# Edge-weighted sums of a graph network on one core: GpSimd makes the target one-hots, ScalarE weighs the rows

## The chip, the cores and the metric

One core of a Trainium2 chip runs the whole program. The metric is the device time in microseconds (us). The kernel before was timed in three runs: 6406.73, 6428.13 and 6429.01, median 6428.13.

## The reference, cut to the sums that the change touches

A four-layer graph network over 6250 nodes with 128 features and 106250 directed edges (100000 drawn plus 6250 self-loops), the edges sorted by target node. The change touches the edge sums of the second layer (L1) only. Cut to what matters there:

```python
edge_feat = jnp.concatenate([x[row], x[col]], axis=-1)
h = jax.nn.gelu(edge_feat @ mlp_w1 + mlp_b1, approximate=False)
edge_weight = jax.nn.sigmoid(h @ mlp_w2 + mlp_b2)[:, 0]
...
deg = jax.ops.segment_sum(ew_f, col_f, num_segments=n)
dinv = jnp.where(deg > 0, jax.lax.rsqrt(deg), 0.0)
norm = dinv[row_f] * ew_f * dinv[col_f]
xt = x @ conv_w
msg = xt[row_f] * norm[:, None]
out = jax.ops.segment_sum(msg, col_f, num_segments=n)
```

Here `row_f` and `col_f` are the edges' sources and targets with the self-loops behind, and `ew_f` their weights. The edge pass before it has computed each edge's weight (`score`) and each node's `dinv`, and has written the gathered rows `xt[row_f]` in edge order to DRAM (`spill`). What is left for the edge sums is, for every edge, weight times `dinv` of its source times its row, added up by target node. The factor `dinv` of the target is applied later, in the node phase.

## The kernel before, in words

Phases follow each other with a barrier between: node phase, attention, node phase, edge pass, `weighted_sums("sum1")` (L901 to L1082), node phase, two plain sums (`convolve`), and so on. `weighted_sums` is called once. The edges lie in 832 tiles of 128 edges; TB = 8 tiles make a batch, so there are 104 batches. One partition holds one edge of a tile. Every engine runs its own list of instructions, and only semaphores order them.

For each batch n:

- **SP** loads the batch's rows from `spill` (L949, 512 KB, three buffers, each free again when `s_wrow` says that its rows have been weighed) and a line with the low seven bits of the source indices, broadcast to all partitions (L941, 256 KB, four buffers, freed by `s_lo`).
- **VectorE** makes a one-hot of those low bits (`low_onehot`, L1027, one instruction for the batch). It is done one batch ahead.
- **TensorE** looks up `dinv` of each source (`look_up`, L981): 24 small bf16 matmuls of the low one-hot with a table of `dinv`, split in three bf16 parts, into `pS`. It is done one batch ahead of the sums.
- **VectorE** picks the right column for each edge (`find`, L1037, eight instructions that also write an accumulated value) and multiplies it by the edge's weight (`weigh_edges`, L1049, "the wedge"; eight values per partition).
- **GpSimd** multiplies the rows by the wedge (L962, one product of 128x1024, into `wrow`). In the first seven batches it also scales the nodes' own rows (`keep`, L967).
- **ScalarE** makes the one-hots of the target nodes (`hot`): eight squares of iota minus the edge's local target (L1012) and then relu(1 - square) over the batch (L1016).
- **TensorE** multiplies (`sum_up`, L993): eight fp32 matmuls of `wrow` with `hot` into `pA`, one for each tile; each shows as two instructions in the trace.
- **VectorE** adds the eight results into `acc` at an address that is read from `base` (`add`, L1057). The adds of batch n-2 stand between the finds of batch n, and each add waits for the one before it (`s_add`). The eight addresses are loaded into registers in front (L1073).

`hot`, `wrow`, `pA`, `hot_lo`, `pS`, `found` and `wedge` have two buffers each. So GpSimd and ScalarE may start on batch n only when the sums of n-2 are done (`s_sum`), and TensorE's sums of n only when the adds of n-2 are done. TensorE's order is look_up(n+1), sum_up(n). VectorE's order in step n is low_onehot(n+1), the address load, eight pairs of find(n) and add(n-2), weigh_edges(n). At the start GpSimd clears `acc` (L955), and VectorE splits `dinv` and the source indices in a chain of seven instructions (L1061 to L1067).

## Time and profile before

| | |
|---|---|
| runs, us | 6406.73, 6428.13, 6429.01 |
| the profiled execution, us | 6410.54 |
| its span, us | 6408.8 |
| stage of the edge-weighted sums, us | about 2475 to 2971 |
| TensorE busy in the span | 3755.1 us (59%) |
| VectorE busy in the span | 3524.7 us (55%) |
| ScalarE busy in the span | 2305.3 us (36%) |
| GpSimd busy in the span | 4226.4 us (66%) |
| mean granted TensorE clock | 0.624 |

The span is the time from the first to the last instruction of the profiled execution; its own time is 1.7 us more. In the rows, L962 is a line of the kernel, PE is TensorE's matmuls and PEld its weight loads, DVE is VectorE, ACT ScalarE, POOL GpSimd and SP the engine that issues most DMAs. A tile such as `wrow` shows as `sum_wrow`. In a row of the timeline the square bracket holds how long the engine was idle before it and what ended that time. The granted clock is 1 at 2.4 GHz and 0.5 at 1.2 GHz. Instructions of one engine overlap a little, so durations can add up to more than the busy time.

### The profile page before, as it was taken

The page shows a single profiled execution, that of the slowest core. Times are in us where ns is not written, and L with a number is a line of the kernel's source. Part 1 is how long each engine was busy: PE and PEld are TensorE (multiplying, and loading weights), DVE is VectorE, ACT ScalarE, POOL GpSimd, SP SyncE. Part 2 cuts the span into 40 slices and gives each one's busy share as a digit, 9 for nine tenths or more (in the row PEclk, how much of TensorE's full clock was granted, in tenths as well). Part 3 has the DMA queues.
Part 4 walks back from the last instruction along what each step waited for, and adds up shares of the span by engine and source line. Part 5 has one row for each costly group of instructions (what it writes and reads, how often), then busy time and mean ns, then how long its engine had stood idle before and what let it go on. Part 6 is the DMA issues. An engine that isn't in the chain of part 4 may idle for free. (4 is left out here: it accounts for less than half of the span.)

```text
span 6408.8 us, 85037 instructions
## 1 busy us (share of the span) xinstructions
PE 3755.1 (59%) x21906; PEld 3499.1 (55%) x21906; DVE 3524.7 (55%) x11783; ACT 2305.3 (36%) x5100; POOL 4226.4 (66%) x4385
## 2 busy tenths in 40 slices
PE   4555555457777776666344444544444456888886
PEld 2555555447777776666333333433333346778776
DVE  4777777655555556886333333333333345666665
ACT  3555555344444445786000000100000026666663
POOL 2777777337777775442777777477777737777773
PEclk8777777656666667898555555655555565555556
DMA  5555555125555555552222222122222213333332
GB/s 152 160 159 160 159 159 160 48 68 156 155 153 156 156 155 156 167 181 87 54 53 53 53 53 53 52 53 53 53 53 53 53 43 61 58 59 59 59 59 49
DMA packets 734950, 621.88 MB, mean 97 GB/s; under 512 B 345701, under 2 KB 625721, under 8 KB 734521
## 3 DMA queue, kind: packets, MB, share of 16 engines
q0 software_dynamic: 159744, 356.39, 21.2%
q1 hardware_dynamic: 574776, 260.77, 15.2%
q8 instruction: 148, 2.42, 0.2%
q14 instruction: 282, 2.30, 0.1%
HBM read 532.40 MB, written 84.29 MB: 96 GB/s over the span
## 5 line engine op out<-in xcount | busy, mean ns | idle before, releaser
L1109 POOL DMA_INDIRECT sum_rows<-tab_row,src_idx x1664 | 1570.0, 944 | 656.4 <-issue 506.4
L1121 PE MATMUL sum_pA<-sum_hot,sum_rows 128*128 128x128 f32 x3328 | 851.2, 437 | 1245.5 <-DVE sum_hot L1131 1149.2
L1121 PEld LDWEIGHTS sum_pA<-sum_hot,sum_rows 128*128 128x128 f32 x3328 | 740.9, 328 | 1355.7 <-DVE sum_hot L1131 1269.4
L1153 DVE TENSOR_TENSOR acc<-acc,sum_pA 128x128 f32 x1664 | 480.8, 289 | 1346.1 <-PE sum_pA L1121 1178.5
L618 POOL DMA_INDIRECT l_rows<-tab_qv,src_idx x832 | 791.0, 951 | 368.4 <-issue 247.4
L618 POOL DMA_INDIRECT l_rows<-tab_wh,src_idx x832 | 787.2, 946 | 349.9 <-issue 249.4
L353 POOL DMA_INDIRECT l_rows<-tab_ax,src_idx x832 | 790.6, 950 | 291.6 <-issue 266.1
L668 PE MATMUL l_pA<-l_hotA,l_wrow 128*128 128x128 f32 x3328 | 708.9, 382 | 58.9 <-DVE acc L854 57.8
L640 PE MATMUL l_pK<-l_winr,l_hotT 128*128 128x128 f32 (+1 forms) x3328 | 665.7, 339 | 69.5 <-DVE l_logit L762 49.2
L640 PEld LDWEIGHTS l_pK<-l_winr,l_hotT 128*128 128x128 f32 x3328 | 636.4, 284 | 80.6 <-issue 52.8
L668 PEld LDWEIGHTS l_pA<-l_hotA,l_wrow 128*128 128x128 f32 x3328 | 641.7, 286 | 70.2 <-issue 40.2
L854 DVE TENSOR_TENSOR acc<-acc,l_pA 128x128 f32 x1664 | 474.1, 285 | 234.1 <-PE l_pA L668 177.2
L697 ACT ACTIVATE l_hot<-iota,local 128x128 bf16<-128x128 f32 x1664 | 525.9, 388 | 13.9 <-PEq L75 13.9
L371 PE MATMUL l_pK<-l_winr,l_hotT 128*128 128x64 f32 x1664 | 339.0, 388 | 237.9 <-ACT l_hotT L410 237.9
L715 ACT ACTIVATE l_hotA<-l_hot 128x512 f32<-128x512 bf16 x416 | 259.6, 624 | 584.1 <-PE l_pA L668 579.0
L371 PEld LDWEIGHTS l_pK<-l_winr,l_hotT 128*128 128x128 f32 x1664 | 320.9, 296 | 255.4 <-ACT l_hotT L410 130.0
L1354 ACT ACTIVATE mid_hT<-mid_pH 128x512 f32<-128x512 f32 x7 | 4.2, 597 | 1078.6 <-PE mid_pH L1311 1078.6
L1329 ACT ACTIVATE gat_rss<-gat_rss 128x7 f32<-128x7 f32 x7 | 1.4, 205 | 1069.7 <-DVE gat_rss L1407 1069.7
L962 POOL TENSOR_TENSOR sum_wrow<-sum_rows,sum_wedge 128x1024 f32<-128x1024 f32 x104 | 214.7, 2064 | 257.0 <-DVE sum_wedge L1049 239.4
L993 PE MATMUL sum_pA<-sum_hot,sum_wrow 128*128 128x128 f32 x1664 | 244.5, 308 | 167.1 <-issue 88.2
L451 DVE TENSOR_TENSOR l_pre<-l_rows,l_pK 128x512 f32<-128x512 f32 x104 | 71.5, 688 | 487.3 <-DMA l_rows<-tab_ax,src_idx 481.6
L993 PEld LDWEIGHTS sum_pA<-sum_hot,sum_wrow 128*128 128x128 f32 x1664 | 224.8, 217 | 175.6 <-issue 174.9
(257 smaller groups left out, 7099.9 us busy)
## 6 DMA issues: line engine op xcount, KB each, us to landing
l_winr<-tab_k SPq DMA_DIRECT2D x832, 64.0 KB
spill<-l_rows SPq DMA_DIRECT2D x104, 512.0 KB
sum_rows<-spill SPq DMA_DIRECT2D x104, 512.0 KB
l_winr<-tab_b SPq DMA_DIRECT2D x840, 32.0 KB
sum_line<-src_lo SPq DMA_DIRECT2D x104, 256.0 KB
sum_rows<-tab_row,src_idx POOLq DMA_INDIRECT x1664
l_rows<-tab_qv,src_idx POOLq DMA_INDIRECT x832
l_rows<-tab_ax,src_idx POOLq DMA_INDIRECT x832
```

The lines of the kernel that those rows point to most:

```text
L353: nc.gpsimd.indirect_dma_start(rows[:, b * TB + u, :], None, table, bass.IndirectOffsetOnAxis(src_idx[:, t:t + 1], 0)).then_inc(s_rows[b], 16)
L371: last = nc.tensor.matmul(pK[:, b, u, :], hotT[:, b, u, :], winr[:, b * TB + u, :], start=True, stop=True)
L618: nc.gpsimd.indirect_dma_start(rows[:, g % R, u, :], None, table, bass.IndirectOffsetOnAxis(src_idx[:, t:t + 1], 0)).then_inc(s_rows[g % R ...
L640: last = nc.tensor.matmul(pK[:, g % 2, u, :], hotT[:, g % 2, u, :], winr[:, g % WR, u, :], start=True, stop=True)
L668: last = nc.tensor.matmul(pA[:, g % 2, u, :], wrow[:, g % 2, u, :], hotA[:, g % 2, u, :], start=True, stop=True)
L697: last = nc.scalar.activation(hot[:, g % HR, u, :], iota[:], ACT.Square, scale=-1.0, bias=local[:, t:t + 1])
L715: nc.scalar.activation(hotA[:, g % 2], hot[:, g % HR], ACT.Copy).then_inc(s_hotA, 1)
L854: nc.vector.tensor_tensor(acc[:, bass.ds(at[u], P)], acc[:, bass.ds(at[u], P)], pA[:, g % 2, u, :], ALU.add).then_inc(s_add, 1)
L993: last = nc.tensor.matmul(pA[:, b, u, :], wrow[:, b, u, :], hot[:, b, u, :], start=True, stop=True)
L1109: nc.gpsimd.indirect_dma_start(rows[:, g % R, u, :], None, tab_row, bass.IndirectOffsetOnAxis(src_idx[:, t:t + 1], 0)).then_inc(s_rows[g % ...
L1121: last = nc.tensor.matmul(pA[:, g % HOTS, u, :], rows[:, g % R, u, :], hot[:, g % HOTS, u, :], start=True, stop=True)
L1153: nc.vector.tensor_tensor(acc[:, bass.ds(at, P)], acc[:, bass.ds(at, P)], pA[:, g % HOTS, u, :], ALU.add).then_inc(s_add, 1)
```

## The change

Five things are changed, all in `weighted_sums`. GpSimd makes the target one-hots, with eight compares (iota equal to the local target) per batch, instead of weighing the rows. ScalarE weighs the rows, with eight scaled copies per batch, instead of making the one-hots. `hot`, `wrow` and `pA` have three buffers instead of two. The adds run three batches behind the finds instead of two, in 107 steps instead of 106. The lookups and the low one-hots run two batches ahead instead of one; the low one-hot now follows the wedge in VectorE's step. The seven `keep` products come in batches 3 to 9 instead of 0 to 6.

```diff
@@ -902,10 +902,10 @@
 
             with Phase(nc) as cx:
                 L = name + "_"
-                RB, LB = 3, 4
-                hot = sb(L + "hot", [P, 2, TB, P], fp32, cx)
+                RB, LB, SB = 3, 4, 3
+                hot = sb(L + "hot", [P, SB, TB, P], fp32, cx)
                 rows = sb(L + "rows", [P, RB, TB, F], fp32, cx)
-                wrow = sb(L + "wrow", [P, 2, TB, F], fp32, cx)
+                wrow = sb(L + "wrow", [P, SB, TB, F], fp32, cx)
                 line = sb(L + "line", [P, LB, TB * P], bf16, cx)
                 hot_lo = sb(L + "hot_lo", [P, 2, TB * P], bf16, cx)
                 picked = sb(L + "picked", [P, 2, TB, NB], fp32, cx)
@@ -915,7 +915,7 @@
                 hi_f = sb(L + "hi_f", [P, T], fp32, cx)
                 part = sb(L + "part", [P, 3, NB], bf16, cx)
                 rest = sb(L + "rest", [P, 2, NB], fp32, cx)
-                pA = ps(cx, L + "pA", [P, 2, TB, P])
+                pA = ps(cx, L + "pA", [P, SB, TB, P])
                 pS = ps(cx, L + "pS", [P, 2, TB, F // 2])[:, :, :, 0:NB]
                 s_rows = [sem(cx, L + f"s_rows{b}") for b in range(RB)]
                 s_line = [sem(cx, L + f"s_line{b}") for b in range(LB)]
@@ -925,7 +925,6 @@
                 s_found = sem(cx, L + "s_found")
                 s_wedge = sem(cx, L + "s_wedge")
                 s_wrow = sem(cx, L + "s_wrow")
-                s_square = sem(cx, L + "s_square")
                 s_hot = sem(cx, L + "s_hot")
                 s_sum = sem(cx, L + "s_sum")
                 s_add = sem(cx, L + "s_add")
@@ -954,17 +953,17 @@
                     def _(pool):
                         nc.gpsimd.memset(acc[:], 0.0).then_inc(s_add, 1)
                         for n in range(BATCHES):
-                            b = n % 2
-                            pool.wait_ge(s_wedge, n + 1)
-                            pool.wait_ge(s_rows[n % RB], 16 * (n // RB + 1))
-                            if n >= 2:
-                                pool.wait_ge(s_sum, n - 1)
-                            nc.gpsimd.tensor_tensor(wrow[:, b], rows[:, n % RB],
-                                                    wedge[:, b].unsqueeze(2).to_broadcast([P, TB, F]), ALU.mult
-                                                    ).then_inc(s_wrow, 1)
-                            if n < GROUPS:
-                                own = keep[:, n * GB:(n + 1) * GB, :]
-                                nc.gpsimd.tensor_tensor(own, own, dinv[:, n * GB:(n + 1) * GB].unsqueeze(2)
+                            if n >= SB:
+                                pool.wait_ge(s_sum, n - SB + 1)
+                            for u in range(TB):
+                                t = n * TB + u
+                                last = nc.gpsimd.tensor_scalar(hot[:, n % SB, u, :], iota[:], local[:, t:t + 1], None,
+                                                               ALU.is_equal)
+                            last.then_inc(s_hot, 1)
+                            if SB <= n < SB + GROUPS:
+                                i = n - SB
+                                own = keep[:, i * GB:(i + 1) * GB, :]
+                                nc.gpsimd.tensor_tensor(own, own, dinv[:, i * GB:(i + 1) * GB].unsqueeze(2)
                                                         .to_broadcast([P, GB, F]), ALU.mult).then_inc(s_scaled, 1)
                         pool.wait_ge(s_scaled, GROUPS)
 
@@ -984,11 +983,11 @@
 
                         def sum_up(n):
 
-                            b = n % 2
+                            b = n % SB
                             pe.wait_ge(s_hot, n + 1)
                             pe.wait_ge(s_wrow, n + 1)
-                            if n >= 2:
-                                pe.wait_ge(s_add, 1 + TB * (n - 1))
+                            if n >= SB:
+                                pe.wait_ge(s_add, 1 + TB * (n - SB + 1))
                             for u in range(TB):
                                 last = nc.tensor.matmul(pA[:, b, u, :], wrow[:, b, u, :], hot[:, b, u, :],
                                                         start=True, stop=True)
@@ -996,25 +995,23 @@
 
                         pe.wait_ge(s_split, 7)
                         look_up(0)
+                        look_up(1)
                         for n in range(BATCHES):
-                            if n + 1 < BATCHES:
-                                look_up(n + 1)
+                            if n + 2 < BATCHES:
+                                look_up(n + 2)
                             sum_up(n)
 
                     @block.scalar
-                    def _(act_e):
+                    def _(ae):
                         for n in range(BATCHES):
-                            b = n % 2
-                            if n >= 2:
-                                act_e.wait_ge(s_sum, n - 1)
+                            ae.wait_ge(s_wedge, n + 1)
+                            ae.wait_ge(s_rows[n % RB], 16 * (n // RB + 1))
+                            if n >= SB:
+                                ae.wait_ge(s_sum, n - SB + 1)
                             for u in range(TB):
-                                t = n * TB + u
-                                last = nc.scalar.activation(hot[:, b, u, :], iota[:], ACT.Square, scale=-1.0,
-                                                            bias=local[:, t:t + 1])
-                            last.then_inc(s_square, 1)
-                            act_e.wait_ge(s_square, n + 1)
-                            nc.scalar.activation(hot[:, b], hot[:, b], ACT.Relu, scale=-1.0, bias=one[:]
-                                                 ).then_inc(s_hot, 1)
+                                last = nc.scalar.activation(wrow[:, n % SB, u, :], rows[:, n % RB, u, :], ACT.Copy,
+                                                            scale=wedge[:, n % 2, u:u + 1])
+                            last.then_inc(s_wrow, 1)
 
                     @block.vector
                     def _(dve):
@@ -1054,7 +1051,7 @@
                             if u == 0:
                                 dve.wait_ge(s_sum, n + 1)
                             dve.wait_ge(s_add, 1 + n * TB + u)
-                            nc.vector.tensor_tensor(acc[:, bass.ds(at, P)], acc[:, bass.ds(at, P)], pA[:, n % 2, u, :],
+                            nc.vector.tensor_tensor(acc[:, bass.ds(at, P)], acc[:, bass.ds(at, P)], pA[:, n % SB, u, :],
                                                     ALU.add).then_inc(s_add, 1)
 
                         c = Chain(dve, s_split)
@@ -1066,20 +1063,21 @@
                         c.link(nc.vector.tensor_scalar(hi_i[:], src_idx[:], 7, None, ALU.logical_shift_right))
                         c.link(nc.vector.tensor_copy(hi_f[:], hi_i[:]))
                         low_onehot(0)
-                        for n in range(BATCHES + 2):
-                            if n + 1 < BATCHES:
-                                low_onehot(n + 1)
-                            if n >= 2:
+                        low_onehot(1)
+                        for n in range(BATCHES + 3):
+                            if n >= 3:
                                 _, at = nc.values_load_multi_w_load_instructions(
-                                    base[0:1, (n - 2) * TB:(n - 1) * TB], engines=[dve.engine], min_val=0, max_val=N,
+                                    base[0:1, (n - 3) * TB:(n - 2) * TB], engines=[dve.engine], min_val=0, max_val=N,
                                     skip_runtime_bounds_check_because="base holds nodes")
                             for u in range(TB):
                                 if n < BATCHES:
                                     find(n, u)
-                                if n >= 2:
-                                    add(n - 2, u, at[u])
+                                if n >= 3:
+                                    add(n - 3, u, at[u])
                             if n < BATCHES:
                                 weigh_edges(n)
+                            if n + 2 < BATCHES:
+                                low_onehot(n + 2)
 
 
         def convolve(name):
```

## Rows read from the trace of the kernel before

**Rows 1.** Windows view: stretch, length, busy us of each engine (count), PEclk, DMA share, GB/s.
```profile
2475.00:2971.00 496.00, 316.71 (x4160) 305.36 (x4160) 421.13 (x2711) 371.41 (x936) 231.57 (x112) 0.89 0.54 167
```

**Rows 2.** Source view of L1049, whole run.
```profile
L1049 DVE TENSOR_TENSOR sum_wedge<-sum_found,score x104: 158/159/255, 2486.5 to 2961.8; 128x8 f32<-128x8 f32 x104
```

**Rows 3.** Waits from 2475 to 2971 us: total us, times, longest.
```profile
ACT sum_hot L1012 <- PE sum_pA L993: 111.2, 78, 10.2
...
DVE sum_picked L1037 <- PE sum_pS L981: 61.1, 78, 2.9
...
DVE acc L1057 <- issue: 2.7, 8, 0.6
...
PE sum_pA L993 <- POOL sum_wrow L962: 78.4, 26, 3.6
```

**Rows 4.** Timeline, one turn of the loop: start us, us, instruction [idle before <- releaser].
```profile
2739.99 0.16 DVE L1049 TENSOR_TENSOR sum_wedge<-sum_found,score 128x8 f32<-128x8 f32 x1
...
2740.23 2.07 POOL L962 TENSOR_TENSOR sum_wrow<-sum_rows,sum_wedge 128x1024 f32<-128x1024 f32 x1 [2.19 <-PE sum_pA L993]
...
2742.40 2.02 PE L993 MATMUL sum_pA<-sum_hot,sum_wrow 128*128 128x128 f32 x16 [1.63 <-issue]
...
2744.26 0.78 PE L981 MATMUL sum_pS<-sum_part,sum_hot_lo 128*128 128x49 bf16 x24
...
2745.08 0.27 DVE L1037 SCALAR_TENSOR_TENSOR sum_picked<-iota,sum_hi_f,sum_pS 128x49 f32<-128x49 f32 x1 [0.38 <-PE sum_pS L981]
```

**Rows 5.** Timeline from 2547 us, VectorE and GpSimd.
```profile
2547.72 0.16 DVE L1049 TENSOR_TENSOR sum_wedge<-sum_found,score 128x8 f32<-128x8 f32 x1
2547.79 0.48 DVE L1027 TENSOR_SCALAR sum_hot_lo<-sum_line,minus_p 128x1024 bf16<-128x1024 bf16 x1
2547.95 2.07 POOL L962 TENSOR_TENSOR sum_wrow<-sum_rows,sum_wedge 128x1024 f32<-128x1024 f32 x1 [3.66 <-DVE sum_wedge L1049]
2548.46 0.27 DVE L1037 SCALAR_TENSOR_TENSOR sum_picked<-iota,sum_hi_f,sum_pS 128x49 f32<-128x49 f32 x1 [0.19 <-issue]
...
2551.84 0.16 DVE L1049 TENSOR_TENSOR sum_wedge<-sum_found,score 128x8 f32<-128x8 f32 x1
```

**Rows 6.** Timeline, sums at the lower clock.
```profile
2632.78 3.41 PE L993 MATMUL sum_pA<-sum_hot,sum_wrow 128*128 128x128 f32 x16 [3.58 <-POOL sum_wrow L962]
```

**Rows 7.** Groups by line on ScalarE; the last row is of the timeline.
```profile
L1012 ACT ACTIVATE sum_hot<-iota,local 128x128 f32<-128x128 f32 x832 | 254.1, 387 | 112.8 <-PE sum_pA L993 111.2 <-PEq L75 1.6
...
L1016 ACT ACTIVATE sum_hot<-sum_hot,one 128x1024 f32<-128x1024 f32 x104 | 119.5, 1149 | 3.4
...
2984.10 2.80 ACT L1334 ACTIVATE gcn_hb<-x_nat,gcn_nbs,gcn_rss 128x128 f32<-128x128 f32 x7 [0.47 <-DVE gcn_nbs L1410]
```

**Rows 8.** GpSimd at 128x128: timeline in the gate phase, then source views.
```profile
1215.64 0.45 POOL L1270 TENSOR_TENSOR gate_tm<-gate_tm,r_beta 128x128 f32<-128x128 f32 x1
1216.05 0.45 POOL L1266 TENSOR_TENSOR gate_tm<-gate_tm,r_gamma 128x128 f32<-128x128 f32 x1
...
L217 POOL TENSOR_SCALAR_AFFINE_SELECT ident<-ident x1: 292/292/292, 1.5 to 1.5; 128x128 f32<-128x128 f32 x1
...
L215 POOL MEMSET ident<- x1: 194/194/194, 1.1 to 1.1; 128x128 f32 x1
```

**Rows 9.** Timeline: VectorE beside GpSimd, stage start and 2709 us.
```profile
2475.34 5.43 POOL L955 MEMSET acc<- 128x6400 f32 x1 [15.69 <-POOLq L75]
...
2475.38 5.44 DVE L1061 CAST sum_part<-dinv 128x49 bf16<-128x49 f32 x1 [0.86 <-PEq L75]
...
2709.00 1.90 POOL L962 TENSOR_TENSOR sum_wrow<-sum_rows,sum_wedge 128x1024 f32<-128x1024 f32 x1 [2.05 <-DVE sum_wedge L1049]
2709.13 2.05 DVE L1027 TENSOR_SCALAR sum_hot_lo<-sum_line,minus_p 128x1024 bf16<-128x1024 bf16 x1 [0.20 <-issue]
```

**Rows 10.** Timeline, the last two groups of additions.
```profile
2962.49 3.22 DVE L1057 TENSOR_TENSOR acc<-acc,sum_pA 128x128 f32 x8 [0.58 <-issue]
2967.64 3.23 DVE L1057 TENSOR_TENSOR acc<-acc,sum_pA 128x128 f32 x8 [1.92 <-PE sum_pA L993]
```

## The prediction

> **What bounds it now.** I first looked for the stage that the change touches. The edge-weighted sums of layer 1 (one call of weighted_sums) run from about 2475 to 2971 us, 496 us of a span of 6408.8; everything outside stays as it is. The stage makes 104 batches. The wedge instruction, one per batch, starts first at 2486.5 and last at 2961.8 [rows 2], so a batch takes 475.3 / 103 = 4.61 us.
>
> No engine is full in that stretch: VectorE is busy 421 of 496 us, ScalarE 371, TensorE 317, GpSimd 232 [rows 1]. So a loop of waits sets the pace, and the waits show it [rows 3]: ScalarE waits 111 us for the sums' matmuls, VectorE 61 us for the lookups' matmuls, TensorE 78 us in 26 long waits for GpSimd's weighted rows. One turn of the loop can be read off the timeline [rows 4]: wedge at 2739.99; GpSimd weighs the rows from 2740.23 for 2.07; the sums' matmuls start at 2742.40 and take 2.02; the lookup two batches later comes behind them on TensorE and ends at 2745.04; VectorE's find starts at 2745.08, and its eight find and add pairs take 3.3 us [rows 5] to the wedge of that batch at about 2748.4. That is 8.4 us for two batches, 4.21 each. When TensorE has waited some 3 us its clock is at the lower of its two levels (1.2 and 2.4 GHz) and the same sums take 3.41 instead of 2.02, as behind the wait of 3.58 [rows 6]. Those turns carry the mean from 4.21 to 4.61: 0.40 x 103 = 41 us in all.
>
> Under the loop lies VectorE's own length. Where find waits for no matmul, two wedges are 2551.84 - 2547.72 = 4.12 us apart [rows 5]: eight pairs, the wedge, the low one-hot, and 0.19 us of "issue" in which it loads the eight addresses. The change leaves all of this in place, so 4.12 is the floor.
>
> **The change, part by part.** The floor of a batch is compared with what each other engine and loop will need.
>
> ScalarE gives up eight squares (about 2.44 us) and the relu (1.15) [rows 7] and gets eight scaled copies of 128x128 from SBUF with one per-partition operand. The trace has no such copy from SBUF. The nearest row is the square, same size and one such operand, 387 ns each, eight in 2.44 us. The far end is the normalising activation with two such operands, seven in 2.80, so eight in 3.2 [rows 7]. I take 2.44, since the operand count is the same. Cheaper than the square I exclude: it is already a plain one-input operation. ScalarE is far under 4.12 either way.
>
> TensorE keeps its work, 2.02 + 0.78 = 2.8 us a batch at the upper clock [rows 4]. The new loop through it is wedge, 2.44 copies, 2.02 sums, 0.78 lookup, 0.1 hand-over, 3.33 pairs = 8.7 us, but the lookups run two ahead, so it spans three batches: 2.9 us each. Even at the lower clock, with 3.41 and at most twice 0.78, it is 10.8 / 3 = 3.6. The additions three behind need the sums 4.6 us after their wedge and come some 8.3 us after it. So the turns at the lower clock, 41 us now, are covered; if that cover went, they would return. The rows' loads wait for the copies instead of GpSimd's product, 0.4 us later, with over two batches in hand; SP's line loads queue behind them as before and have more. The bytes are the same in less time: 167 GB/s becomes about 184. No row of waits names a DMA, so I put this at nothing.
>
> GpSimd gives up the 2.07 us product and gets eight compares of 128x128 with one per-partition operand. This price no row shows. From below: a memset of 128x128 takes 0.19 and affine_select 0.29. From above: the two-input product of that size takes 0.45 and consecutive ones start 0.41 apart (1215.64 to 1216.05) [rows 8]. The compare reads one tile, like affine_select, so I take 0.30, 2.4 us a batch; with 0.41 it is 3.3. Both lie under 4.12. A compare dearer than a product can't be excluded and is a rival. The batch's seven keep products move three batches later and stay in GpSimd's slack.
>
> VectorE shares something with GpSimd. A cast of 49 columns lasted 5.44, beside GpSimd's memset of 5.43; a low one-hot of normally 0.48 that came 0.13 after GpSimd's product had begun lasted 2.05, until the product was over [rows 9]. Find and add run on at 0.42 a pair beside the product that starts at 2547.95 [rows 5]. So low one-hot (and casts, and the wedge perhaps) wait for the GpSimd instruction under way. Today they nearly always start first. The Trainium skill says so too: "Advanced Engine Details and Errata", section Mode Summary, has GpSimd instructions and VectorE's two-port modes block each other. The trace agrees for the low one-hot, 2.05 us against 0.48, while find and add kept their pace. By that rule in its mildest form, one wait of half a compare, a batch gains 0.15 us; by the phases below it gains nothing.
>
> Will they meet in the new order? GpSimd may start the compares of batch k+3 when the sums of k end, 2.44 + 2.02 + 0.1 = 4.6 us after wedge k. With 2.4 of work it is done at 7.0, with 3.3 at 7.9. Wedge k+2 comes at 8.3. They miss each other while TensorE's clock is up. At the lower clock they meet: a wait of at most one compare, 0.3, for one or two instructions.
>
> **Sum.** Prologue: nine short VectorE instructions now run beside GpSimd's first 24 compares, each waiting 0 to 0.4; I take 2 us in all. First wedge at 2486.5 + 2 = 2488.5. Wedge 3 must wait for the first copies, the sums at the lower clock, lookup 3 (between 0.78 and twice that) and the pairs: 2.5 + 3.5 + 1.2 + 3.3 = 10.5, so 2499.0. Then 100 batches at 4.12, plus 0.03 for the odd stall (2.7 us of "issue" over 104 batches [rows 3]) = 4.15: wedge 103 at 2914.0. Then three groups of additions instead of two: 0.73 to the first, 3.22 each, 0.6 between [rows 10] = 11.6, so 2925.6, against 2967.64 + 3.23 = 2970.9. Saved: 45 us, 0.7%. The profiled execution (6410.5, its span plus 1.7) becomes 6365. The runs' median is 6428.1, 17.6 above it, and would become 6383. The times shown run from 6406.7 to 6429.0, so I forecast between the two, 6375 (6420 before, less 45).
>
> **Rivals.** First, **the two engines meet in every batch**. Then the compares delay wedge k+2, and two batches last 4.6 + 8 compares: (4.6 + 3.7) / 2 = 4.15 even at 0.46 a compare, but with the dearer copies (3.2) and 0.45 it is 4.5; with 0.55 a compare and the cheap copies, 4.5. Or the phase settles differently and every batch pays one and a half compares of 0.3, giving 4.6. Against it: the phase worked out above keeps them apart. For it: wherever they met, VectorE waited for the whole of GpSimd's instruction. At 4.5 the saving is 10 us: 6410. Chance 0.18.
>
> Second, **GpSimd becomes the bound**. Place: the compares at L962 of the new kernel. If one costs over 0.5 us, eight pass VectorE's floor; with about 0.2 for the low one-hot, a batch is 8c + 0.2. It equals today's 4.61 at c = 0.55; slower by over 0.5% it is from a batch of 4.92, c = 0.59. At c = 0.65 the batch is 5.4 and the stage loses 80 us net: 6500. For it: no compare with a pointer operand ran on GpSimd in this trace. Against it: all five kinds there at this size lie at or under 0.45. The Trainium skill warns here: "GPSIMD Engine Reference", Engine selection, keeps elementwise work off GpSimd, though it calls one-input work about line rate there. Chance 0.10.
>
> Third, **the time at the lower clock stays on the path**: the gaps on TensorE now are 1.3 us instead of up to 3, so this needs a wait that I don't see. With a tenth of the batches at 5.6 the saving is 30 us: 6390. Chance 0.07, inside the range.
>
> My forecast case has 0.65. **Range**: the low end is the floor of 4.12, no prologue cost and a run like the lowest, 6406.7 - 45 - 5 = 6357, put at 6355; the high end takes in the meeting case from a run like the highest, 6429 - 10, put at 6420. Outside lies mostly the second rival. **Chances**: 0.5% is 32 us, about what a measurement of this kernel tells from none, and needs a batch under 4.28. Faster: 0.65 + the third rival's half and a little of the first = 0.71; same 0.19; slower 0.10.
>
> **What the new profile should show.** Wedges 4.15 apart; find waiting for lookups hardly at all, 61 us before; ScalarE's copies near 387 ns; GpSimd's compares 0.3 apart, then idle for the sums; the low one-hot at 0.48 in most batches; TensorE's clock over 0.95 where it was 0.89 [rows 1]. Wedges over 4.3 with the low one-hot near 0.8 would mean the first rival, GpSimd without idle time the second. A stage of 496 us or more would prove me wrong.

## The result and the profile after

The changed kernel took 6444.43 us in the median of eight runs (6440.68 to 6449.43), the kernel before 6425.69 in the median of eight (6406.73 to 6432.7). The ratio is 1.0031, with a 95% interval of 1.002 to 1.0042: slower by about 19 us, where 45 us less were forecast. The profiled execution took 6440.74 us, its span 6439.0. That is 30 us more than the profiled execution of the kernel before, which was one of its shorter ones; 28 of the 30 lie in the stage of the edge-weighted sums. Its row in the windows view, to be held against [rows 1]:

```profile
2475.00:3002.00 527.00, 364.48 (x4166) 348.47 (x4167) 438.19 (x2712) 254.30 (x832) 517.23 (x840) 0.78 0.51 157
```

The stage is 527 us long instead of 496. GpSimd is busy 517 of them (232 before), ScalarE 254 (371 before), and TensorE's granted clock is 0.78, where it was 0.89. The groups by line show why (out<-in, count, then busy us, mean ns, and idle time in front with what ended it):

```profile
L960 POOL TENSOR_SCALAR sum_hot<-iota,local 128x128 f32<-128x128 f32 x832 | 500.4, 620 | 0.0
...
L992 PE MATMUL sum_pA<-sum_hot,sum_wrow 128*128 128x128 f32 x1664 | 283.5, 340 | 147.0 <-POOL sum_hot L960 146.0 <-ACT sum_wrow L1012 1.0
...
L1012 ACT ACTIVATE sum_wrow<-sum_rows,sum_wedge 128x128 f32<-128x128 f32 x832 | 254.3, 388 | 260.5 <-DVE sum_wedge L1046 260.5
...
L1024 DVE TENSOR_SCALAR sum_hot_lo<-sum_line,minus_p 128x1024 bf16<-128x1024 bf16 x104 | 61.5, 593 | 0.4 <-issue 0.4
...
L1046 DVE TENSOR_TENSOR sum_wedge<-sum_found,score 128x8 f32<-128x8 f32 x104 | 27.8, 267 | 0.3 <-issue 0.2
```

A compare on GpSimd, L960, lasts 620 ns on the mean by its own record (596 in the median), and GpSimd is never idle in front of one. ScalarE's copies last 388 ns, as forecast, and ScalarE now idles 260 us for the wedge. VectorE's low one-hot lasts 593 ns on the mean, 526 before, and the wedge 267 instead of 160. The waits of the stage (total us, times, longest) say who is late:

```profile
ACT sum_wrow L1012 <- DVE sum_wedge L1046: 260.5, 102, 13.3
...
PE sum_pA L992 <- POOL sum_hot L960: 146.0, 101, 3.9
DVE sum_picked L1034 <- PE sum_pS L980: 73.9, 62, 2.6
```

TensorE's sums now wait for GpSimd's one-hots in practically every batch: 146 us, 101 times. In [rows 3] they had waited 78 us, 26 times, for the weighted rows, and the waits view of before, from 2475 to 2971 us, has a second row for them:

```profile
PE sum_pA L993 <- issue: 88.2, 63, 1.9
```

So TensorE idled even longer in front of the sums before, 167 us in all. What is new is who ends each of these waits, and that GpSimd never rests. The timeline shows the pace:

```profile
2739.94 22.82 POOL L960 TENSOR_SCALAR sum_hot<-iota,local 128x128 f32<-128x128 f32 x38
...
2740.01 2.05 PE L992 MATMUL sum_pA<-sum_hot,sum_wrow 128*128 128x128 f32 x16 [0.54 <-POOL sum_hot L960]
...
2744.79 3.27 PE L992 MATMUL sum_pA<-sum_hot,sum_wrow 128*128 128x128 f32 x16 [2.12 <-POOL sum_hot L960]
...
2749.60 2.05 PE L992 MATMUL sum_pA<-sum_hot,sum_wrow 128*128 128x128 f32 x16 [0.59 <-POOL sum_hot L960]
```

Thirty-eight compares follow each other in 22.8 us, 0.60 us each, without a gap. The sums start 4.78 and 4.81 us apart, each released by the eighth compare of its batch. After 2.12 us of idling the sums at 2744.79 run mostly at the lower clock (0.59 granted) and take 3.27 us; it costs nothing here, since the next compares are not ready.

### The profile page after: what moved, and what is told of

It is laid out like the page before. It is cut to its first block and busy times, and to the rows that moved or that the text cites. A ratio compares the mean times of both kernels' runs of the same rounds, so it can differ in the third digit from the quotient of the medians.

```text
span 6439.0 us, 85661 instructions
## 1 busy us (share of the span) xinstructions
PE 3806.2 (59%) x21906; PEld 3544.3 (55%) x21906; DVE 3538.6 (55%) x11783; ACT 2188.3 (34%) x4996; POOL 4512.2 (70%) x5113
## 5 line engine op out<-in xcount | busy, mean ns | idle before, releaser
L618 POOL DMA_INDIRECT l_rows<-tab_qv,src_idx x832 | 791.6, 951 | 368.3 <-issue 245.0
L618 POOL DMA_INDIRECT l_rows<-tab_wh,src_idx x832 | 786.5, 945 | 350.4 <-issue 247.9
L353 POOL DMA_INDIRECT l_rows<-tab_ax,src_idx x832 | 790.8, 951 | 291.3 <-issue 266.7
L960 POOL TENSOR_SCALAR sum_hot<-iota,local 128x128 f32<-128x128 f32 x832 | 500.4, 620 | 0.0
L992 PE MATMUL sum_pA<-sum_hot,sum_wrow 128*128 128x128 f32 x1664 | 283.5, 340 | 147.0 <-POOL sum_hot L960 146.0
L992 PEld LDWEIGHTS sum_pA<-sum_hot,sum_wrow 128*128 128x128 f32 x1664 | 259.1, 245 | 159.1 <-POOL sum_hot L960 158.0
L1012 ACT ACTIVATE sum_wrow<-sum_rows,sum_wedge 128x128 f32<-128x128 f32 x832 | 254.3, 388 | 260.5 <-DVE sum_wedge L1046 260.5
```

The source lines that it names most:

```text
L353: nc.gpsimd.indirect_dma_start(rows[:, b * TB + u, :], None, table, bass.IndirectOffsetOnAxis(src_idx[:, t:t + 1], 0)).then_inc(s_rows[b], 16)
L618: nc.gpsimd.indirect_dma_start(rows[:, g % R, u, :], None, table, bass.IndirectOffsetOnAxis(src_idx[:, t:t + 1], 0)).then_inc(s_rows[g % R ...
L960: last = nc.gpsimd.tensor_scalar(hot[:, n % SB, u, :], iota[:], local[:, t:t + 1], None, ALU.is_equal)
L992: last = nc.tensor.matmul(pA[:, b, u, :], wrow[:, b, u, :], hot[:, b, u, :], start=True, stop=True)
```

## The experiments

They ran on other chips. There the kernel before takes 7737 to 7830 us, so each is compared by its ratio with the kernel before on the same chip. Run e9 shows that the stage in question is the same there: engine instructions have the same durations (the product 2071 ns in the median against 2070, the square 386 in both), and the added time lies in the stages that gather rows. From the first to the last of GpSimd's indirect loads, the four stages with L353, L618 (twice) and L1109 are together 1355 us longer, of 1413 in all.

**e1: the old roles with the new depth.** GpSimd's product and ScalarE's squares and relu come back, with three buffers, additions three behind and lookups two ahead.

```diff
--- the changed kernel
+++ e1
@@ gpsimd
+                            pool.wait_ge(s_wedge, n + 1)
+                            pool.wait_ge(s_rows[n % RB], 16 * (n // RB + 1))
                             if n >= SB:
                                 pool.wait_ge(s_sum, n - SB + 1)
-                            for u in range(TB):
-                                t = n * TB + u
-                                last = nc.gpsimd.tensor_scalar(hot[:, n % SB, u, :], iota[:], local[:, t:t + 1], None,
-                                                               ALU.is_equal)
-                            last.then_inc(s_hot, 1)
+                            nc.gpsimd.tensor_tensor(wrow[:, n % SB], rows[:, n % RB],
+                                                    wedge[:, n % 2].unsqueeze(2).to_broadcast([P, TB, F]), ALU.mult
+                                                    ).then_inc(s_wrow, 1)
...
```

> The old roles (GpSimd weighs the rows with one product, ScalarE makes the one-hots), with only the new depth: three buffers, additions three behind, lookups two ahead. Theory A, GpSimd's eight compares are the new bound and the depth is right: without the compares the batch falls to VectorE's floor, 4.15 us, the stage to about 450 us and the time 45 us below the kernel before, near 6380. Theory B, the depth itself does not help or harms: the batch stays at 4.6 us or above and the time at 6425 or more. Theory C, VectorE waiting for GpSimd's instructions at the wedge and the low one-hot is what costs: with a product of 1.9 us that starts after the wedge as before, the low one-hot stays near 0.5 us and the result is that of A.

Measured: 7711.11 us against 7759.02, ratio 0.9935 (0.9914 to 0.9955). Its rows: the wedge, the stretch from the first to the last wedge in the windows view, and two waits.

```profile
L1050 DVE TENSOR_TENSOR sum_wedge<-sum_found,score x104: 159/159/257, 3149.2 to 3582.4; 128x8 f32<-128x8 f32 x104
...
3149.20:3582.40 433.20, 298.04 (x4096) 272.13 (x4096) 408.88 (x2662) 361.72 (x909) 224.24 (x110) 0.97 0.60 185
...
PE sum_pS L981 <- DVE sum_hot_lo L1028: 39.6, 93, 2.2
...
DVE sum_picked L1038 <- issue: 19.3, 97, 0.5
```

From 3149.2 to 3582.4 a batch takes 4.21 us; in the timeline 67 of the 103 intervals are 4.11 to 4.14. The clock is 0.97. Find waits for no lookup any more, only 0.2 us per batch of "issue", the address load; TensorE waits for VectorE's low one-hot instead. So theory A holds and B falls: VectorE's floor of 4.12 [rows 5] is what is left.

**e2: the new roles with the old depth.** The kernel before, with the eight compares on GpSimd and the eight scaled copies on ScalarE exactly as in the change, two buffers, additions two behind and lookups one ahead.

```diff
--- the kernel before
+++ e2
@@ gpsimd
-                            pool.wait_ge(s_wedge, n + 1)
-                            pool.wait_ge(s_rows[n % RB], 16 * (n // RB + 1))
                             if n >= 2:
                                 pool.wait_ge(s_sum, n - 1)
-                            nc.gpsimd.tensor_tensor(wrow[:, b], rows[:, n % RB],
-                                                    wedge[:, b].unsqueeze(2).to_broadcast([P, TB, F]), ALU.mult
-                                                    ).then_inc(s_wrow, 1)
+                            for u in range(TB):
+                                t = n * TB + u
+                                last = nc.gpsimd.tensor_scalar(hot[:, b, u, :], iota[:], local[:, t:t + 1], None,
+                                                               ALU.is_equal)
+                            last.then_inc(s_hot, 1)
...
```

> The old depth (two buffers, additions two behind, lookups one ahead), with only the roles swapped. Theory A: eight compares of 0.595 us make 4.76 us a batch and GpSimd is still always busy, so the time is that of the changed kernel within 10 us, 6440 to 6455. Theory B (the new depth is what costs): with the old depth the time falls back to the kernel before, 6425, or below.

Measured: 7823.23 us, ratio 1.0083 (1.0059 to 1.0107). The time did not fall back, so B is out; but it is not that of the changed kernel either, it is some 35 us worse. A miss for A.

```profile
L1046 DVE TENSOR_TENSOR sum_wedge<-sum_found,score x104: 159/160/1341, 3144.5 to 3679.8; 128x8 f32<-128x8 f32 x104
...
PE sum_pA L992 <- ACT sum_wrow L1012: 138.8, 40, 4.6
DVE sum_picked L1034 <- PE sum_pS L980: 110.5, 57, 4.6
POOL sum_hot L961 <- PE sum_pA L992: 25.7, 41, 1.3
```

A batch takes (3679.8 - 3144.5) / 103 = 5.20 us. GpSimd idles 25.7 us for the sums, which the third buffer of the changed kernel takes away, and TensorE waits 139 us for the copies, VectorE 110 us for the lookups: the old two-batch loop, now with copies of 2.44. At the lower clock it is 2.5 + 3.4 + 1.2 + 3.3 = 10.4 us for two batches, 5.2 each. The sum fits: in the timeline intervals of some 4.1 and some 6.2 us alternate, and two neighbours add up to 10.36 in the median. It was not tested apart.

**e3: six compares on GpSimd, two one-hots on ScalarE.** In the changed kernel, GpSimd's loop runs to TB - 2 and ScalarE makes the last two, in front of its wait for the wedge.

```diff
--- the changed kernel
+++ e3
@@ gpsimd
-                            for u in range(TB):
+                            for u in range(TB - 2):
@@ scalar
+                            if n >= SB:
+                                ae.wait_ge(s_sum, n - SB + 1)
+                            for u in range(TB - 2, TB):
+                                t = n * TB + u
+                                last = nc.scalar.activation(hot[:, n % SB, u, :], iota[:], ACT.Square, scale=-1.0,
+                                                            bias=local[:, t:t + 1])
+                            last.then_inc(s_square, 1)
+                            ae.wait_ge(s_square, n + 1)
+                            nc.scalar.activation(hot[:, n % SB, TB - 2:TB, :], hot[:, n % SB, TB - 2:TB, :], ACT.Relu,
+                                                 scale=-1.0, bias=one[:]).then_inc(s_hot2, 1)
                             ae.wait_ge(s_wedge, n + 1)
...
```

> The changed kernel with six of the eight one-hots of a batch made by GpSimd and two by ScalarE (square and relu) before its copies. Theory A: GpSimd needs 6 x 0.595 = 3.6 us, ScalarE 0.6 + 0.4 + 2.4 = 3.4, so VectorE's floor of 4.12 decides, and a batch takes 4.15 to 4.3: 30 to 45 us below the kernel before. Theory C, VectorE's waits for the GpSimd instruction under way decide: GpSimd is still busy nine tenths of the time, each batch pays about 0.45 us over 4.12, and the time stays within 10 us of the kernel before.

Measured: 7726.97 us, ratio 0.995 (0.9931 to 0.9969).

```profile
L1057 DVE TENSOR_TENSOR sum_wedge<-sum_found,score x104: 158/159/1484, 3153.4 to 3591.2; 128x8 f32<-128x8 f32 x104
...
L962 POOL TENSOR_SCALAR sum_hot<-iota,local 128x128 f32<-128x128 f32 x624 | 369.3, 611 | 59.1 <-PE sum_pA L995 59.1
```

The batch is (3591.2 - 3153.4) / 103 = 4.25 us. Taking a quarter of the compares away turned the loss into most of the gain, although GpSimd is still busy 375 us of 438 and the compare costs the same 611 ns. That speaks for A and against C, which asked for 0.45 us a batch over 4.12. With idle time on GpSimd the low one-hot is back at 0.481 us in the median, so in most batches the two no longer meet.

**e4: the prices alone.** In the kernel before, behind its first block, GpSimd runs a row of instructions back to back into scratch.

```diff
--- the kernel before
+++ e4
+                    for i in range(3):
+                        nc.gpsimd.tensor_scalar(acc[:, 0 + i * 128:128 + i * 128], iota[:], local[:, 0:1], None, ALU.is_equal)
+                    for i in range(3):
+                        nc.gpsimd.tensor_scalar(acc[:, 384 + i * 128:512 + i * 128], iota[:], 3.0, None, ALU.is_equal)
+                    for i in range(3):
+                        nc.gpsimd.tensor_scalar(acc[:, 768 + i * 128:896 + i * 128], iota[:], local[:, 1:2], None, ALU.mult)
...
+                    for i in range(3):
+                        nc.gpsimd.tensor_tensor(acc[:, 2752 + i * 128:2880 + i * 128], iota[:], ident[:], ALU.mult)
```

> The kernel before with a row of GpSimd instructions alone behind its first block, back to back into scratch: prices only. If the compare's price is a matter of the pointer operand, the compare with a constant falls from 0.60 to 0.45 us or less; if of the operation, the multiplication with the pointer operand does; if of a fixed cost per instruction, 64 columns cost nearly as much as 128 and 512 columns under 1.2 us; if of each element, 64 columns cost 0.35 and 512 about 2 us. The two-input product of 128 columns should be 0.41 apart as before, the two-input subtraction of 1024 columns 1.9.

Measured in its one run, by line (L261 the kernel's compare, L263 the same with a constant, L265 a multiplication with a pointer operand, L269 the compare over 64 columns, L271 over 512, L273 the two-input product, L274 a two-input subtraction over 1024, both inputs broadcast views, L275 a compare with a constant over 1024):

```profile
L271 POOL TENSOR_SCALAR acc<-x_nat,local 128x512 f32<-128x512 f32 x2 | 3.1, 1552 | 0.0
...
L275 POOL TENSOR_SCALAR acc<-x_nat 128x1024 f32<-128x1024 f32 x1 | 2.8, 2757 | 0.0
L274 POOL TENSOR_TENSOR acc<-iota,local 128x1024 f32<-128x1024 f32 x1 | 1.9, 1886 | 0.0
L261 POOL TENSOR_SCALAR acc<-iota,local 128x128 f32<-128x128 f32 x3 | 1.8, 605 | 40.5 <-PEq L257 40.5
L265 POOL TENSOR_SCALAR acc<-iota,local 128x128 f32<-128x128 f32 x3 | 1.8, 598 | 0.0
...
L263 POOL TENSOR_SCALAR acc<-iota 128x128 f32<-128x128 f32 x3 | 1.5, 518 | 0.0
L273 POOL TENSOR_TENSOR acc<-iota,ident 128x128 f32<-128x128 f32 x3 | 1.3, 446 | 0.0
L269 POOL TENSOR_SCALAR acc<-iota,local 128x64 f32<-128x64 f32 x3 | 1.3, 434 | 0.0
```

The compare's 0.605 us depend neither on the operation (0.598 for the multiplication) nor much on the pointer (0.518 with a constant). From 64 over 128 to 512 columns it takes 0.434, 0.605 and 1.552 us: 2.5 ns a column and 0.28 us fixed. The two-input product goes from 0.446 at 128 to 1.886 at 1024: 1.6 ns a column. So the instruction with one tile and a scalar is the dearer one per column, the other way round than I had it. So neither the operation nor the pointer explains the price as the expectation had it; 512 columns lie between its two cases for them, 1.2 us for a fixed cost and 2 us for a cost per element.

**e5: subtractions in place of the compares.** The changed kernel with another instruction in the same 832 places. It makes no one-hot, so its sums are of other numbers.

```diff
--- the changed kernel
+++ e5
-                                last = nc.gpsimd.tensor_scalar(hot[:, n % SB, u, :], iota[:], local[:, t:t + 1], None,
-                                                               ALU.is_equal)
+                                last = nc.gpsimd.tensor_tensor(hot[:, n % SB, u, :], iota[:],
+                                                               local[:, t:t + 1].to_broadcast([P, P]), ALU.subtract)
```

> The changed kernel with each of GpSimd's 832 compares replaced by a two-input subtraction of the same 128 columns, which the kernel before's rows price at 0.41 us apart instead of 0.595; the one-hot is not made, so the sums of layer 1 and all that follows are of other numbers. Theory A, only the compare's price was wrong in the forecast: 8 x 0.41 = 3.3 us a batch is under VectorE's floor, the batch becomes 4.15 to 4.2 and the time 40 to 48 us below the kernel before (ratio 0.993 to 0.995). Theory C, GpSimd's instructions delay the wedge and the low one-hot whenever they are many and short: VectorE waits about 0.4 us per batch, the batch stays near 4.6 and the ratio near 1.000.

Measured: 7719.8 us against 7758.69, ratio 0.9954 (0.9931 to 0.9978).

```profile
L1046 DVE TENSOR_TENSOR sum_wedge<-sum_found,score x104: 157/159/830, 3154.3 to 3587.9; 128x8 f32<-128x8 f32 x104
...
L960 POOL TENSOR_TENSOR sum_hot<-iota,local 128x128 f32<-128x128 f32 x832 | 304.9, 402 | 119.0 <-PE sum_pA L992 119.0
```

The batch is (3587.9 - 3154.3) / 103 = 4.21 us, as in e1. Everything of the change is in this kernel but GpSimd's instruction, so the rest of the forecast held: with the price that I had assumed as the far end, the batch is near VectorE's floor. GpSimd has idle time again (119 us, for the sums), and the low one-hot again lasts 0.480 us in the median. So e5 takes away two things at once, the compare's price and the meetings of the two engines; the next section parts them. The ratio lies a little over the band that A gave; the interval reaches into it.

**e6 and e7: the depth in its two halves.** e6 is the kernel before with the lookups and low one-hots two ahead and nothing else.

```diff
--- the kernel before
+++ e6
@@ tensor
                         look_up(0)
+                        look_up(1)
                         for n in range(BATCHES):
-                            if n + 1 < BATCHES:
-                                look_up(n + 1)
+                            if n + 2 < BATCHES:
+                                look_up(n + 2)
@@ vector
                         low_onehot(0)
+                        low_onehot(1)
                         for n in range(BATCHES + 2):
-                            if n + 1 < BATCHES:
-                                low_onehot(n + 1)
...
                             if n < BATCHES:
                                 weigh_edges(n)
+                            if n + 2 < BATCHES:
+                                low_onehot(n + 2)
```

> The kernel before with only the lookups and low one-hots two batches ahead; two buffers, additions two behind and the old roles stay. If the loop of 4.21 us (wedge, product, sums, lookup behind the sums, find) was what held the kernel before, this alone opens it: 4.15 to 4.25 us a batch at the upper clock, ratio 0.993 to 0.995. If two buffers hold it as well (the additions of n-2 need sums that end 4.2 us after their wedge, or 5.6 at the lower clock), the slow turns stay and the ratio is 0.997 to 1.000.

Measured: 7719.27 us, ratio 0.9939 (0.9918 to 0.9959).

```profile
L1050 DVE TENSOR_TENSOR sum_wedge<-sum_found,score x104: 157/159/257, 3149.4 to 3587.1; 128x8 f32<-128x8 f32 x104
...
3149.40:3587.10 437.70, 294.25 (x4095) 267.57 (x4096) 409.68 (x2672) 366.43 (x918) 224.26 (x110) 0.98 0.59 184
```

A batch takes (3587.1 - 3149.4) / 103 = 4.25 us. e7 is the kernel before with third buffers for `hot`, `wrow` and `pA` and the additions three behind, lookups still one ahead.

```diff
--- the kernel before
+++ e7
-                hot = sb(L + "hot", [P, 2, TB, P], fp32, cx)
+                hot = sb(L + "hot", [P, SB, TB, P], fp32, cx)
...
-                                    add(n - 2, u, at[u])
+                                    add(n - 3, u, at[u])
```

> The kernel before with only the third buffers and the additions three batches behind; lookups one ahead and the old roles stay. The loop through the lookup is still closed over two batches, 4.21 us at the upper clock and more at the lower, so the ratio stays at 0.998 to 1.001. If the buffers were what held the kernel before, it falls to 0.994.

Measured: 7769.14 us (twelve runs, one of them 11066.83), ratio 0.9999 (0.9976 to 1.0022).

```profile
L1049 DVE TENSOR_TENSOR sum_wedge<-sum_found,score x104: 159/159/253, 3141.1 to 3604.8; 128x8 f32<-128x8 f32 x104
...
3141.10:3604.80 463.70, 299.08 (x4096) 288.74 (x4096) 404.45 (x2663) 361.33 (x909) 224.37 (x110) 0.92 0.56 173
```

4.50 us a batch in this trace, against 4.65 in that of e9. The runs show no gain clear of their noise, so nearly all of the depth's gain comes from putting the lookup, and with it the low one-hot, one batch earlier; the loop ran through TensorE's order, as [rows 4] had it, and not through the buffers.

**e8: addresses loaded sixteen at a time**, in e1. It asks whether VectorE's own instructions are the floor.

```diff
--- e1
+++ e8
-                            if n >= 3:
+                            if n >= 3 and (n - 3) % 2 == 0:
-                                _, at = nc.values_load_multi_w_load_instructions(
-                                    base[0:1, (n - 3) * TB:(n - 2) * TB], engines=[dve.engine], min_val=0, max_val=N,
+                                _, ats = nc.values_load_multi_w_load_instructions(
+                                    base[0:1, (n - 3) * TB:(n - 1) * TB], engines=[dve.engine], min_val=0, max_val=N,
...
-                                    add(n - 3, u, at[u])
+                                    add(n - 3, u, ats[(n - 3) % 2 * TB + u])
```

> The kernel of e1 (old roles, new depth), with the addresses loaded sixteen at a time every second batch instead of eight in every batch. If VectorE's own instructions are what holds e1 at 4.12 us in most batches, a batch with no load in front loses the 0.19 us of issue and the batches alternate between about 3.95 and 4.15: 4.10 to 4.12 on the mean against 4.21, some 10 us in all, which the wedges' spacing shows and the time hardly. If something else holds it (the rows' loads, or GpSimd's product), the spacing stays at 4.12 and find waits instead.

Measured: 7782.48 us against 7810.12, ratio 0.996 (0.9947 to 0.9974).

```profile
L1050 DVE TENSOR_TENSOR sum_wedge<-sum_found,score x104: 157/159/254, 3182.2 to 3623.2; 128x8 f32<-128x8 f32 x104
...
L1073 DVEq TENSOR_LOAD <-base x52: 1095/1099/1116, 3188.1 to 3626.4; - x52
```

The batches do alternate, so VectorE is the floor, but at other values than expected: 38 intervals are 3.79 or 3.80 us and 26 are 4.62 or 4.63. The mean of the two, 4.21, is no better than 4.12, and with intervals of 4.76 and 4.98 in between the mean of all is (3623.2 - 3182.2) / 103 = 4.28, where e1 has 4.21. A load costs 4.12 - 3.79 = 0.33 us of the batch, not 0.19, and one of sixteen 0.83. In the kernel before a load of eight takes, on VectorE's sequencer,

```profile
L1073 DVEq TENSOR_LOAD <-base x104: 593/596/601, 2488.7 to 2965.4; - x104
```

0.596 us, against 1.099 here: the load grows with the number of addresses, and the low one-hot covers only the first part of it.

**e9: the kernel before, on these chips.**

> The kernel before, unchanged, for its trace on the chips of the experiments, where the whole program takes 1.2 times as long. Its stage should be as in the first trace, 4.5 to 4.65 us a batch with the same durations, since no row of it waits for a transfer; the added time must lie in the stages that gather rows.

```profile
L1049 DVE TENSOR_TENSOR sum_wedge<-sum_found,score x104: 157/159/253, 3191.2 to 3670.0; 128x8 f32<-128x8 f32 x104
...
3191.20:3670.00 478.80, 315.74 (x4096) 304.69 (x4096) 406.46 (x2670) 364.06 (x918) 224.24 (x110) 0.88 0.55 168
```

7823.46 us in its one run. Between the wedges it takes 478.8 us, 4.65 a batch, clock 0.88; 475.3 in the first trace. The added time lies outside this stage.

**e10: the changed kernel, on these chips.**

> The changed kernel, unchanged, on the chips of the experiments, beside e2, which swaps the roles alone. If GpSimd's compares hold both, the batch is 4.85 us as in its first trace and the loss some 25 us, a ratio of 1.002 to 1.004; the 5.2 us of e2 would then be the price of the old depth under the new roles.

Measured: 7846.88 us against 7810.12, ratio 1.0041 (1.0026 to 1.0056), and 4.85 us a batch:

```profile
L1046 DVE TENSOR_TENSOR sum_wedge<-sum_found,score x104: 157/172/2026, 3183.1 to 3683.0; 128x8 f32<-128x8 f32 x104
```

It confirms the loss, and sets the price of the old depth under the new roles (e2) at 5.20 - 4.85 = 0.35 us a batch, 36 us.

## Why the prediction was wrong, point by point

**The bound before** was read rightly. The loop wedge, product, sums, lookup, find was cut by e6 alone, and the batch fell from 4.65 (e9) to 4.25 us. With the old roles the depth brought what was forecast: 48 us less in e1.

**VectorE's floor of 4.12** held: 67 intervals of e1 lie there, and e5 reached 4.21 on the mean. The forecast's 4.15 was 0.06 short, 6 us over 103 batches; in e1, e3 and e5 some twelve intervals of 4.48, 0.35 too long, make 4 us. What stalls VectorE there was not looked into.

**ScalarE's copy** was taken as 387 ns; it is 388.

**The compare is the step that failed.** The term "eight compares of 0.30 us, 2.4 a batch; with 0.41 it is 3.3" is mis-sized. A compare measures 0.596 us by its record, and a compare that nothing disturbs starts 0.577 after the one before, 4.62 a batch:

```profile
L960 POOL TENSOR_SCALAR sum_hot<-iota,local x832: 591/596/1166, 2481.7 to 2993.0; 128x128 f32<-128x128 f32 x167
...
L1024 DVE TENSOR_SCALAR sum_hot_lo<-sum_line,minus_p x104: 480/572/940, 2484.4 to 2978.1; 128x1024 bf16<-128x1024 bf16 x104
...
L1046 DVE TENSOR_TENSOR sum_wedge<-sum_found,score x104: 157/182/2016, 2487.8 to 2986.9; 128x8 f32<-128x8 f32 x104
```

(count: shortest/median/longest ns; first and last start.) My bound from above was the two-input product, on the thought that one input can't cost more than two; affine_select was the nearest row for no better reason than that it reads one tile. e4 shows that the instruction with a scalar costs 2.5 ns a column and the product 1.6. VectorE's one-input shift over 832 columns costs 0.7 ns a column in the trace before:

```profile
L1066 DVE TENSOR_SCALAR sum_hi_i<-src_idx 128x832 int32<-128x832 int32 x1 | 0.6, 594 | 0.0
```

The Trainium skill, "GPSIMD Engine Reference", section Engine selection, calls one-input work on GpSimd roughly line rate; the 2.5 ns a column of e4 beside VectorE's 0.7 contradict it for this instruction. Its advice in the same table, elementwise work to VectorE, no run here tests.

**The meeting of VectorE and GpSimd** was forecast not to happen while TensorE's clock is up. It happens in nearly every batch, as GpSimd never rests, and it is a second step that failed. One meeting, in the timeline and in the source view of L960 over 2738.1 to 2738.6 and 2738.9 to 2742.5:

```profile
2737.55 0.29 DVE L1046 TENSOR_TENSOR sum_wedge<-sum_found,score 128x8 f32<-128x8 f32 x1
2737.77 0.57 DVE L1024 TENSOR_SCALAR sum_hot_lo<-sum_line,minus_p 128x1024 bf16<-128x1024 bf16 x1
...
L960 POOL TENSOR_SCALAR sum_hot<-iota,local x1: 758/758/758, 2738.0 to 2738.0; 128x128 f32<-128x128 f32 x1
...
L960 POOL TENSOR_SCALAR sum_hot<-iota,local x7: 595/595/596, 2738.8 to 2742.2; 128x128 f32<-128x128 f32 x7
```

Both sides lose. The wedge and the low one-hot take 0.29 and 0.57 us instead of 0.16 and 0.48. The compare that starts during the low one-hot takes 0.758 instead of 0.595, and the seven behind it start 0.577 apart. In the trace's records 105 of the 832 compares last over 0.7 us, and 104 of these overlap a low one-hot. What VectorE loses costs nothing here, for the wedge is not the bound. What GpSimd loses is on the path: 0.16 us a batch, 17 us in all. The last three batches meet no low one-hot, and they are 4.62 long where the others are 4.78 in the median. The first rival had the meeting but the wrong side of it: it priced the delay of VectorE. The nine instructions of the prologue lose some 0.5 us together instead of 2 (the chain's product at 2481.84 takes 0.33, 0.21 before).

The Trainium skill's rule in "Advanced Engine Details and Errata", section Mode Summary, that the two block each other, holds for the product and the memset [rows 9]. Beside the `keep` products the wedge was held too, up to 2.0 us. For the compares the trace agrees as well, but a meeting costs either side under 0.5 us, since each compare is short: from the wedge's start to the low one-hot's end it is 0.74 us in the median, 0.56 in the trace before.

**The keep products** were to stay in GpSimd's slack. There was none, so they lengthen the stage by seven times 1.68 us, 12 us:

```profile
L966 POOL TENSOR_TENSOR keep<-keep,dinv x7: 1677/1681/1685, 2502.1 to 2541.1; 128x896 f32<-128x896 f32 x7
```

**The stage's length** then follows from GpSimd alone: memset 5.4, then 832 compares and seven keep products from 2481.7 to 2993.6, the last sums at the lower clock and the last additions:

```profile
2481.84 0.33 DVE L1059 TENSOR_TENSOR sum_rest<-dinv,sum_part 128x49 f32<-128x49 f32 x1
...
2984.88 8.68 POOL L960 TENSOR_SCALAR sum_hot<-iota,local 128x128 f32<-128x128 f32 x15
...
2993.61 2.95 PE L992 MATMUL sum_pA<-sum_hot,sum_wrow 128*128 128x128 f32 x16 [2.56 <-POOL sum_hot L960]
2996.70 3.23 DVE L1054 TENSOR_TENSOR acc<-acc,sum_pA 128x128 f32 x8 [1.20 <-PE sum_pA L992]
```

From 2476.32, when the stage's memset starts in this trace, to 2996.70 + 3.23 are 523.6 us; before it was 495.5. The 28 us between them are, within a microsecond, the meetings (17) and the keep products (12). The bare compares, 4.62 a batch, only equal the 4.61 of before: their price took the gain away, and the other two made the loss.

**The second rival** had this mechanism, its place and its threshold: from 0.55 us a compare no gain. Its formula, 8c + 0.2, gives 4.82 a batch with the spacing of 0.577, and 4.78 were measured; so its 0.2 for the low one-hot was nearly right. It left out the keep products. It had a chance of 0.10 where the unknown price deserved a range reaching past 0.45, since no row had that instruction.

**The lower clock**: TensorE fell to 0.78, against a forecast over 0.95. That was a result of GpSimd's being the bound: e1, e5 and e6 without the compares have 0.97 or 0.98, and e3 with six of them 0.96.

## What to carry to other kernels

When a change moves work to an engine on which no row shows that instruction, the forecast hangs on that one price: time a few of them alone first, at the size and with the operand kinds that the kernel uses, since fewer inputs need not mean less time. In a loop of waits over several batches, look for the one edge that closes it; here looking up one batch earlier was worth the whole 0.6%, and the buffers nothing that the runs could tell from noise. And when an engine becomes the bound, everything that it had done in its idle time, and every wait for a neighbour, is added to the path. The best version measured keeps the old roles and only looks up two batches ahead (e6, 0.9939; with the buffers too, e1, 0.9935).

## What the runs showed that I had not expected

GpSimd's instruction with one tile and a per-partition scalar costs more per column (2.5 ns) than its two-input product (1.6 ns), and a pointer operand adds 0.09 us over a constant. VectorE's low one-hot waits for the whole of a GpSimd product that has begun, and a cast lasted as long as GpSimd's memset; beside back-to-back compares the wedge and the low one-hot lose 0.2 us together, and the GpSimd compare that starts during the low one-hot loses 0.16, 0.758 instead of 0.595. Loading addresses into VectorE's registers takes 0.60 us for eight and 1.10 for sixteen, so batching the loads saves nothing. No single gap tells at which clock TensorE runs next. In the changed kernel the sums at 2759.18 came after only 1.09 us of idling and ran at the lower clock, 3.60 us (granted 0.54), those at 2740.01 after 0.54 at the upper one; the kernel before kept the upper one with gaps of 1.6.
